# The halves of h turned by DMA in pairs of tiles, the squares of the spline weights inside the counting, five PSUM banks for the attention sums

## The reference

```python
def reference(x, src, dst, W0, a, base_w, spline_w, W, b, gamma, beta):   # names shortened
    h = relu(layernorm(x))                         # x: 1250 x 512; 20,000 edges src, dst, sorted by dst
    # layer 0: attention over the edges, then a spline layer
    HW = h @ W0
    s, t = HW @ a[:512, 0], HW @ a[512:, 0]
    e = leaky_relu(s[src] + t[dst], 0.2)
    ex = exp(e - segment_max(e, src)[src])
    att = ex / segment_sum(ex, src)[src]
    agg = segment_sum(att[:, None] * h[dst], src)
    basis = b_splines(agg, grid)                   # 8 functions for each entry
    x = x + silu(agg) @ base_w.T + einsum('nip,oip->no', basis, spline_w)
    h = relu(layernorm(x))
    # layer 1: three rounds of a graph convolution with self loops, batch norm and relu
    for l in range(3):
        y = h @ W[l].T
        agg = segment_sum(y[src] * norm[:, None], dst) + b[l]
        h = relu(gamma[l] * batchnorm(agg) + beta[l])
    return x + h
```

## Time and profile before

| | us |
|---|---|
| median of three runs | 618.08 |
| the three runs | 620.51, 612.05, 618.08 |
| the profiled execution | 613.95 |
| its span | 611.8 |

### The profile page before, as it was taken

The page is one execution under the profiler, slowest core; times in us unless marked ns, Lnnn a source line. Parts: engine busy times, 40 slices in busy tenths (PEclk is TensorE's granted clock), DMA queues, the critical chain, the costliest instruction groups (busy, mean ns, idle before and its releaser), DMA issues.

```text
span 611.8 us, 9451 instructions
## 1 busy us (share of the span) xinstructions
PE 578.0 (94%) x3797; PEld 379.8 (62%) x3797; DVE 435.9 (71%) x717; ACT 332.7 (54%) x420; POOL 42.9 (7%) x40
## 2 busy tenths in 40 slices
PE   4998949999989999999999999999999999999994
PEld 2766848889645555555555555687557855587552
DVE  7999699997679999993499779362474335542555
ACT  4568466569999989891898234044132333142112
POOL 1056100000000000000000030042000020000000
PEclk9999779999998999999999999999999999999998
DMA  9960078662600000000000001240200000000112
GB/s 306 356 239 2 3 180 186 142 90 50 237 1 0 2 2 0 1 1 0 1 2 1 1 1 43 91 193 0 70 1 0 1 1 2 1 0 1 41 43 84
DMA packets 40459, 36.36 MB, mean 59 GB/s; under 512 B 28414, under 2 KB 30078, under 8 KB 40288
## 3 DMA queue, kind: packets, MB, share of 16 engines
q1 hardware_dynamic: 40416, 35.76, 19.5%
HBM read 23.36 MB, written 5.84 MB: 48 GB/s over the span
## 4 chain that ended last, share of the span: by engine, by line
PE 80%; DVE 13%; ACT 2%; issue 2%; DMA 1%; DVEq 1%; ACTq 0%
PE bank L1689 36%; PE bank L1774 21%; PE bank L1731 13%; PE bank L1647 2%; DVE MSK L1140 2%; DVE EX L1153 2%; PE bank L1569 2%; DVE HL L1169 2%; DVE EX L1157 1%; PE bank L1652 1%; DVE OR L1013 1%; DVE BHL L1239 1%; PE bank L1558 1%; PE bank L1524 1%; DMA AT<-HL 1%
## 5 line engine op out<-in xcount | busy, mean ns | idle before, releaser
L1689 PE MATMUL bank<-BHL,WKh 128*128 128x418 f16 x1152 | 206.4, 341 | 2.1 <-DVE BHL L1239 2.1
L1689 PEld LDWEIGHTS bank<-BHL,WKh 128*128 128x128 f16 x1152 | 111.7, 97 | 96.2 <-DVE BHL L1239 2.5
L1774 PE MATMUL bank<-C,YH 128*128 128x418 f16 x360 | 122.4, 340 | 0.0
L1774 PE MATMUL bank<-C,YL 128*128 128x418 f16 x360 | 122.3, 340 | 0.0
L1470 DVE SCALAR_TENSOR_TENSOR Z<-bank,yback,dvb 128x418 f32<-128x418 f32 x36 | 23.4, 651 | 52.1 <-PE bank L1774 52.1
L950 ACT ACTIVATE bnc<-bnm,tiny 128x1 f32<-128x1 f32 x12 | 3.5, 296 | 91.7 <-DVE bnm L1478 91.7
L1774 PEld LDWEIGHTS bank<-C,YH 128*128 128x128 f16 x360 | 35.3, 98 | 28.8 <-issue 0.8
L1647 PE MATMUL bank<-AT,hH 128*128 128x256 f16 (+1 forms) x200 | 45.8, 277 | 7.7 <-DMA AT<-HL 7.7
L1774 PEld LDWEIGHTS bank<-C,YL 128*128 128x128 f16 x360 | 35.2, 98 | 28.0
L912 ACT ACTIVATE YH<-bank,dvl 128x512 f16<-128x512 f32 x30 | 20.4, 686 | 56.6 <-PE bank L1731 56.6
L1416 DVE SCALAR_TENSOR_TENSOR YL<-bank,dvl,YH 128x512 f16<-128x512 f32 x30 | 22.0, 749 | 39.1 <-ACT YH L912 39.1
(11 more groups left out here) (220 smaller groups left out, 963.7 us busy)
## 6 DMA issues: line engine op xcount, KB each, us to landing
WKf<-in_wk SPq DMA_DIRECT2D x9, 1024.0 KB, 6.6
c_scratch<-C SPq DMA_DIRECT2D x10, 320.0 KB, 3.0
C<-c_scratch SPq DMA_DIRECT2D x1, 3200.0 KB, 10.3
GWf<-in_gwT SPq DMA_DIRECT2D x3, 1024.0 KB, 11.5
XT<-in_xT SPq DMA_DIRECT2D x1, 2500.0 KB, 9.3
outT<-Z SPq DMA_DIRECT2D x3, 625.0 KB, 3.0
hx<-in_x SPq DMA_DIRECT2D x1, 1280.0 KB, 6.9
Wt<-in_WT SPq DMA_DIRECT2D x1, 1024.0 KB, 9.1
```

What stands on the lines that cost most here:

```text
L1689: ins = mm(bank[:, 4 * (g % 2) + o, 0:G], lhs, rhs, start=(u == 0 and q == 0 and i == 0), stop=(u == UNITS - 1 and q == PAIR - 1 and i == 2))
L1774: ins = mm(bank[:, u % YB, 0:G], Y[:, j, o * P:(o + 1) * P], C16[:, j, g * G:(g + 1) * G], start=(j == 0 and i == 0), stop=(j == NT - 1 an ...
```

## The change

- ACT rounds hH behind `activations(t)` (at group `H_AT[t]`), DVE subtracts hL one group later; GpSimd has no part in it any more.
- PE turns no tile of h. SP turns hH and hL by DMA transposes, a pair of tiles at once (128 x 1024, 256 KB), into hT in fp16. PE then multiplies hT with the two columns of the attention vector, split in fp16 halves (wsplit): `rows(b)` gives `trow` at once for a set of tiles, `cols(b)` the columns st. The columns are scaled to a norm of 64 (`bounds`), and the exponential takes the scale back; the shift of SHIFTED is the constant 1480. DVE makes the sums that need the columns in `source_columns()`.
- SP loads four WKf blocks first, and one of the other five behind each pair's two transposes.
- `block_squares(i)` runs in groups 10 to 18 of the counting, its trace is read behind group 19.
- The sums of attention go round five banks, 3 to 7; the spline layer's first unit waits for 19 evictions.
- The writes of C16 begin after tile 1's transposes and not after tile 0's; the scale of the weights is computed at tile 4 and not 6.

```diff
-TURN_AT = (5, 6, 8, 9, 11, 12, 14, 15, 16, 17)
-ROUND_AT = 2
+H_AT = (5, 6, 7, 8, 9, 11, 12, 13, 14, 15)
+ROWS_IN = (12, 17, 19)
+COLS_IN = (13, 18, 19)
+H_SETS = ((0, 4), (4, 8), (8, 10))
+SUM_BANKS = 5
-ROWS_AT = (11, 17)
+ROWS_AT = (14, 19)
+WK_FIRST = 4
+SQUARES_AT = 10
...
-            return bank[:, 4 + k, 0:width_of(i)]
+            return bank[:, 3 + (DC * i + k + 2) % SUM_BANKS, 0:width_of(i)]
...
-            for i in range(KB):
+            def spline_weights(i):
                 if i >= 2:
                     sp.wait_ge(wk_in(i - 2), wk_count(i - 2))
                 sp.dma_start(WKf[:, i, :].rearrange("p (c o) -> p c o", c=DC),
                              wk[i * D:(i + 1) * D, :].rearrange("(c p) o -> p c o", p=P)).then_inc(wk_in(i), 16)
+
+            for i in range(WK_FIRST):
+                spline_weights(i)
             sp.dma_start(gpar[:, :, :, :], gvec).then_inc(gpar_in, 16)
+            sp.wait_ge(wa_done, 1)
+            for b, (t0, t1) in enumerate(H_SETS):
+                for t in range(t0, t1, 2):
+                    for k, (half, set_) in enumerate(((hH, h_high), (hL, h_low))):
+                        sp.wait_ge(set_, t + 2)
+                        sp.dma_start(hT[:, k, t:t + 2, :, :].rearrange("p t c n -> p (t c) n"),
+                                     half[:, t:t + 2, :].rearrange("p t d -> p (t d)"), transpose=True).then_inc(hT_in[b], 16)
+                    spline_weights(WK_FIRST + t // 2)
...
-                for t in range(2 * s, min(2 * s + 2, NT)):
+                for t in range(2 * s - 2, 2 * s) if 1 <= s <= NT // 2 else ():
                     sp.dma_start(c16_dram[:, t, :], C16[:, t, :]).then_inc(c16_out, 16)
...
-            for t in range(NT):
-                pool.wait_ge(h_high, t + 1)
-                nc.gpsimd.tensor_tensor(hL[:, t, :], hx[:, t, :], hH[:, t, :], ALU.subtract).then_inc(h_low, 1)
...
+            def rounded(t):
+                act.wait_ge(h_rows, t + 1)
+                nc.scalar.copy(hH[:, t, :], hx[:, t, :]).then_inc(h_high, 1)
...
                 for t in range(NT):
-                    if n == TURN_AT[t] - 1:
+                    if n == H_AT[t]:
                         activations(t)
+                        rounded(t)
                 for b in range(2):
                     if n == ROWS_AT[b]:
                         rows_low(b)
+            rows_low(2)
             columns_out()
-            rows_low(2)
...
-            def rounded(t):
-                dve.wait_ge(h_rows, t + 1)
-                V.tensor_copy(hH[:, t, :], hx[:, t, :]).then_inc(h_high, 1)
+            def low_half(t):
+                dve.wait_ge(h_high, t + 1)
+                V.tensor_tensor(hL[:, t, :], hx[:, t, :], hH[:, t, :], ALU.subtract).then_inc(h_low, 1)
...
                 for t in range(NT):
-                    if n == TURN_AT[t] + ROUND_AT:
-                        rounded(t)
+                    if n == H_AT[t] + 1:
+                        low_half(t)
+                if n == SQUARES_AT + SQUARE_BLOCKS:
+                    block_squares()
+                    dve.wait_ge(sq_read, 1)
+                    V.tensor_copy(wsc[:, 0:1], wss[:, 0:1]).then_inc(sumsq_set, 1)
...
+            def rows(b):
+                t0, t1 = H_SETS[b]
+                pe.wait_ge(hT_in[b], 16 * (t1 - t0))
+                pe.wait_ge(wn_set, 1)
                 for c in range(DC):
-                    ins = nc.tensor.transpose(bank[:, 3, c * P:(c + 1) * P], hx[:, t, c * P:(c + 1) * P], ident[:, :])
-                ins.then_inc(h_turned, 1)
...
+                    for i, k in ((0, 0), (1, 0), (0, 1)):
+                        ins = mm(trow[:, t0 * P:t1 * P], down(wsplit[:, i, c, 1:2]), hT[:, k, t0:t1, c, :],
+                                 start=(c == 0 and i + k == 0), stop=(c == DC - 1 and k == 1))
+                ins.then_inc(rows_in, 1)
+
+            def cols(b):
+                for t in range(*H_SETS[b]):
+                    for c in range(DC):
+                        for k in range(2):
+                            ins = mm(bank[:, 2, ST_AT + 2 * t:ST_AT + 2 * t + 2], hT[:, k, t, c, :],
+                                     wsplit[:, 0:2 + k:1 + k, c, 0], start=(c == 0 and k == 0),
+                                     stop=(c == DC - 1 and k == 1))
+                ins.then_inc(cols_in, 1)
...
+                if SQUARES_AT <= n < SQUARES_AT + SQUARE_BLOCKS:
+                    block_squares(n - SQUARES_AT)
...
-            for i in range(SQUARE_BLOCKS):
-                block_squares(i)
...
-                    if i >= 1:
-                        pe.wait_ge(agg_out, DC * (i - 1) + k + 1)
+                    if i == 0 and k == DC - 1:
+                        pe.wait_ge(deg_read, 1)
+                    if DC * i + k >= SUM_BANKS:
+                        pe.wait_ge(agg_out, DC * i + k - SUM_BANKS + 1)
                     attend(i, k)
...
+            pe.wait_ge(agg_out, DC * len(GROUP_TILES) - 1)
             silu_units(0)
```

More of the change, by code:

```diff
@@ L628, in statistics @@
                     act.wait_ge(x_in, 32)
[L629 removed]
+                nc.scalar.activation(JST[:, :], hx[:, t, :], ACT.Identity, accum_out=mv[:, 0, t:t + 1])
                 act.drain()
@@ L668, in vectors @@
                 both = bank[:, 2, WA_AT:WA_AT + 2 * DC].rearrange("p (c k) -> p c k", k=2)
-                nc.scalar.copy(wcol[:, :, 0:2], both)
-                nc.scalar.mul(wcol[:, :, 2:3], both[:, :, 0:1], BEND)
-                nc.scalar.mul(wcol[:, :, 3:4], both[:, :, 0:1], -BEND).then_inc(wa_set, 1)
-                act.wait_ge(wa_set, 1)
-                nc.scalar.activation(wjunk[:, :], wcol[:, :, 1:2].rearrange("p c k -> p (c k)"), ACT.Square,
-                                     accum_out=wsum[:, 0:1]).then_inc(wa_squared, 1)
+                nc.scalar.copy(wraw[:, :, :], both).then_inc(wa_set, 1)
+                nc.scalar.activation(wjunk[:, :, :].rearrange("p c k -> p (c k)"), bank[:, 2, WA_AT:WA_AT + 2 * DC],
+                                     ACT.Square, accum_out=wsum[:, 0:1]).then_inc(wa_squared, 1)
             def vector_bound():
@@ L722, in exponential @@
                 act.wait_ge(exp_bias, s + 1)
-                nc.scalar.activation(ex(s), ex(s), ACT.Exp, bias=bex[:, s:s + 1]).then_inc(exps, 1)
+                nc.scalar.activation(ex(s), ex(s), ACT.Exp, bias=bex[:, s:s + 1], scale=bnd[:, 0:1]).then_inc(exps, 1)
             def weight_high(s):
@@ L1591, in _ @@
                     mm(bank[0:1, 0, 0:1], ones[:, 0:1], flag[:, 0:1], start=True, stop=True).then_inc(rises_done, 1)
-                if n == TURN_AT[0] + 2:
-                    pe.wait_ge(ctl_set, 1)
-                for t in range(NT):
-                    if n == TURN_AT[t] + 2:
-                        row_spread(t)
-                for t in range(NT):
-                    if n == TURN_AT[t]:
-                        turn(t)
-                for t in range(NT):
-                    if n == TURN_AT[t] + 1:
-                        dots(t)
+                if SQUARES_AT <= n < SQUARES_AT + SQUARE_BLOCKS:
+                    block_squares(n - SQUARES_AT)
+                for b in range(len(H_SETS)):
+                    if n == ROWS_IN[b]:
+                        pe.wait_ge(ctl_set, 1)
+                        rows(b)
+                    if n == COLS_IN[b] and b == 2:
+                        pe.wait_ge(sumsq_set, 1)
+                        mm(bank[:, 2, SUM_AT:SUM_AT + 1], ones[:, :], wsc[:, 0:1], start=True, stop=True).then_inc(sumsq_done, 1)
+                    if n == COLS_IN[b]:
+                        cols(b)
             pe.wait_ge(ctl_set, 1)
```

151 lines of the change are left out of this document (66 added, 85 removed).

## The result

The changed kernel takes 623.3 us, median of 4 runs (622.96 to 623.77). The kernel before took 615.33 us, median of the 4 runs beside them (612.05 to 620.51). The ratio is 1.0138, 95% interval 1.0092 to 1.0184: slower by 1.4%, within the 2% that the prediction took as no change. The profiled execution took 623.77 us (span 622.0), against 613.95 (611.8): 9.8 us more, where my sum had 9.4.

The account below looks back on a forecast made before the run. DVE was taken to bind the counting, and the DVE and ACT chain the end. +9.0 + 0.7 - 0.3 = +9.4 us gave 623.4 profiled and 627.5 on the median; the forecast was the middle, 625.5 us, range 615 to 633.

Parts of the forecast that it names:

- The sum: Whole kernel: +9.0 us at the first `largest`, +0.7 for `source_columns()`, -0.3 in attention, together +9.4 us.
- Part 1: Counting: low halves go from GpSimd to DVE, high halves from DVE to ACT; DVE alone -5.3 us, but then waits for hH.
- Sum -5.3: alone, DVE would end the counting at 56.9 us in place of 62.2: Counting: stretched OMs -8.7, casts -3.5, subtractions +6.0, longer `bounds()` +0.9 us on DVE.
- Part 2: PE in the counting: squares 1.6 or 0.85 us a block, first `rows` 3.9 us, DVE waiting 3.9 us for tile 7's rounding.
- The rest at 2.4 GHz: PE in the counting: after the first `rows`, all its work would run at the higher clock.
- rival (a): PE's clock stays or falls to 1.2 GHz in groups 13 to 19: +3 to +6 us, so 629 to 632; chance 0.22.
- Part 3: SP queue: WKf loads wait behind transposes of hH and hL, 1.45 us per 256 KB; WKf 8 lands at about 71.0 us.
- It lands at about 71.0 us. PE has reached the squares of block 8 by 67 and waits: End of counting: WKf 8's late load stops PE before the last squares, a wait of 2 to 4 us.
- Part 4: Counting's tail: `largest(0)` starts at 76.0 us in place of 66.98, +9.0; `source_columns()` adds 0.7 us before the first EX.
- Part 5: Attention and spline: DVE -0.3 us, fifth bank 0, the wait for 19 evictions 2.2 us but covered, leaving +0.1.
- The -0.3 in attention: Attention: DVE no longer reads the squares at tile 4, which saves 0.3 us.
- the fifth bank gives 0: Attention's sums: a unit may start before its predecessor but three is evicted; PE never waited for agg_out, so 0 gain.

Follow-up runs that it names:

- run 11: Changed kernel with low halves two groups after rounding, all WKf loads first, squares after the degrees, four banks, first `rows` in group 15: 610.77 us, ratio 0.9964.
- run 12: The kernel of run 11 with the squares of WKf put back into groups 10 to 18 of the counting: 613.19 us, ratio 0.9998.
- Run 5: Kernel before, with only hH rounded by ScalarE and hL subtracted by VectorE three groups later, nothing on GpSimd: 622.3 us, ratio 1.01.
- Run 6: Changed kernel with 12 extra matmuls, results thrown away, behind the counts of each of groups 14 to 17: 622.98 us, ratio 1.0145.
- run 1: Changed kernel with VectorE's low halves two groups after ScalarE's rounding in place of one: 622.57 us, ratio 1.0118.
- run 7: Changed kernel with the subtractions for hL back on GpSimd: 623.09 us, ratio 1.0163.
- run 2: Changed kernel with all nine loads of WKf issued ahead of the first transpose: 620.81 us, ratio 1.0119.
- run 8: Changed kernel with the constant 0.031 as the exponential's scale in place of a column: 622.25 us, ratio 1.0115.
- run 4: Changed kernel with four banks for the sums and no wait of the first spline unit for the nineteenth eviction: 621.21 us, ratio 1.009.
- run 10: Changed kernel with all loads of WKf first and four banks for the sums: 621.59 us, ratio 1.0122.
- run 9: Changed kernel with low halves one group later, loads first, squares after the degrees, four banks, one SHIFTED and LOW a group sooner: 616.4 us, ratio 1.003.
- run 3: Changed kernel with the squares of WKf after the degrees and four banks for the sums: 617.8 us, ratio 1.0078.

## Why the prediction was right, and where it was not

**The sum.** +9.4 predicted, +9.8 measured (+10.2 in the spans); by the medians +8.0, and the 623.3 us lie inside the range. First largest +9.0 predicted, +8.5 measured. The 623.4 that the sum gave for the profiled execution came closer than the 625.5 of the forecast, which leaned on where the kernel before would lie. The nearness is in part luck: the terms below miss both ways.

**Part 1, what held.** The stretching went (OM 0.48 us throughout), the subtraction is 0.60 us to the next start as taken from the earlier trace rows, and VectorE waits for hH in the places named: 0.78, 2.23, 1.46, 1.88 and 0.79 us. Only tile 7's was half of the 3.9 predicted. "Sum -5.3: alone, DVE would end the counting at 56.9 us in place of 62.2" was near as the time of a VectorE that nothing holds: in runs 11 and 12, with one wait for hH of 0.2 us, the last OM ended at 57.87 and 57.84. **What failed** is its reading as a gain that part 1 brings. Run 5 made just that exchange in the kernel before, VectorE waited 6.7 us for hH, and the first largest came 2.4 us later. The term prices VectorE with nothing to wait for. The prediction put the waits back in for the change, one group apart, but took three groups' distance as enough.

**Part 2.** The squares of a block took 1.67 us to the next start at the lower clock and 0.92 at the higher (1.6 and 0.85 predicted), and the clock rose near 49 us (50 predicted); the first `rows` took 2.75 us, not 3.9, as it began after the rise. "The rest at 2.4 GHz" failed: rival (a) came true for 59 to 70 us, in groups 16 and 17 and not in the tail. It cost 2.0 us in `rows` and 0.8 in each of two blocks of squares.

**Part 3.** "It lands at about 71.0 us. PE has reached the squares of block 8 by 67 and waits" is the step that failed in its place, though the mechanism was right. The load was issued at 63.64 (64.5 predicted). TensorE waited one load sooner, 0.72 us for block 7, which stands behind the pair 6 and 7 in the same queue, then lost its time in the slow `rows` and came to block 8 at 70.42, without a wait. The loads of blocks 6 to 8 landed 5.6 to 6.2 us after their issue, so block 8 was there by 69.9; the sum had added 2.4 us of transposes to 5.5, and that was too much. Run 6 took the clock's share away and uncovered the predicted wait at 68.99; runs 1 and 7 freed VectorE and uncovered waits of 6.7 and 7.0 us. Rows at the lower clock and the wait for WKf lie over one another, so neither alone gives back its price. Count(19) ended at 72.8, near the 73.4 predicted, by two errors that met.

The price of a transpose can be read from run 2, in a window with the last two of them (issued at 59.25 and 60.53) and no load: PE, PEld, DVE, ACT and POOL busy, granted clock, DMA share, GB/s.
```profile
59.00:64.00 5.00, 3.48 (x59) 2.72 (x55) 4.74 (x6) 1.52 (x3) 0.00 (x0) 1.00 0.55 105
```
0.55 of 5 us is 1.38 us for each 256 KB, near the 1.45 that the sum took. The Trainium skill (DMA: Bandwidth & Descriptors, section Latency and other measured facts) gives 261 GB/s for a DMA transpose with a non-contiguous middle dimension and some 350 to 400 GB/s for a contiguous one. By the first, 256 KB are an estimate of 1.0 us. The window doesn't agree with either, and the measurement stands.

**Part 4.** From count(19) to the first largest 2.7 us (2.6 predicted), and 0.64 us for `source_columns`: right.

**Part 5.** The -0.3 in attention was +1.14 besides `source_columns`, so this term missed by 1.4 us. The sum left out the exponential's column scale, 0.73 us (run 8). The rest was not tested apart; the two operations on mx with bnd's columns take 0.21 us in place of 0.15, which makes 0.11 us a tile on VectorE. That the fifth bank gives 0 held: no wait for agg_out stands between the sums. The wait for 19 evictions was 3.7 us and not 2.2, and cost 0.3 where I took 0.1 (run 4). That the old gap's fall of the clock is exchanged for the new one's also held in this trace, -0.07 us for the whole rest. This is one outcome of several, since the clock can hold in either gap (run 4).

**Which part made it slower.** By run 11 against the change, in the counting it is not the new work itself but the places it was given: low halves a group too near, loads queued behind waits for hH, and squares between the last counts. Each moved alone gives back 0.7 to 3.4 us by the medians. Together, with four banks and with the first `rows` moved as the loads then ask for, it is 12.5 us, of which 12.0 lie at the first largest. The attention's share, 1.8 us, is the new work's own and stays (2.1 in run 11).

## What to carry to other kernels

When work moves between engines that hand each other one group after another, price it on the receiving engine too, and look for waits between them even where the distance seems ample. A load queued behind transposes that wait for computed data inherits those waits; put it ahead, and then look which consumer of the transposes now comes too early. When one cure gives nothing, look for a second wait that lies over the first before calling the cause disproved.

## What the runs showed of the hardware

TensorE's clock fell in some executions and held in others across the same gaps of 1.31 and 0.68 us behind the same counts. It fell to 1.2 GHz in the change at 59.3 (granted 0.55 from 59 to 61 us), in run 4 at 59.3 (0.51) and in run 10 at 60.0 (0.50). It held in run 2 at 58.5 and in run 8 at 58.9 (both 1.00); in run 8 it fell after the next gap, of 1.52 us. With 48 small matmuls more, 12 in each of four groups, it stayed up in the one execution profiled (run 6). After the wait of 2.1 to 2.2 us in the spline it fell in the kernel before and in runs 5, 9 and 10, and held in runs 3, 4, 11 and 12; the difference was 1.6 us.

A queue's issue time is a cost too. A transpose of hL that came 2.5 to 2.8 us behind a 1 MB load held SP's queue 3.1 to 3.9 us (run 1), and one that came 5 us or more behind it 1.3 us (the change). In both, and in runs 6 and 7, the long issues ended 5.9 to 6.8 us after the load's issue, about when such a load lands (6.2 us, the change's median).

An activation of 1280 columns with columns for both scale and bias took 1.45 us, with a constant scale 1.36.
